# Copying the router's columns of the folded value weights with ScalarE instead of a second pair of DMAs, and the order of the SBUF tiles

## The reference

```python
nx = layer_norm(x) * gamma + beta
q, k, v = nx @ Wq, ctx @ Wk, ctx @ Wv
weights = softmax(q k^T * H**-0.5)                 # [b, t, 64]
evidence = weights @ v
combined = concat([nx, evidence, anchor], -1)      # 768 features
router_probs = softmax(combined @ router_W + router_b)
h = silu(combined @ e_w1[e] + e_b1[e])             # three experts, 512 each
routed = sum_e router_probs[e] * (h @ e_w2[e] + e_b2[e])
g = sigmoid(silu(combined @ gate_w1 + gate_b1) @ gate_w2 + gate_b2)
out = x + g * (routed @ out_w + out_b)
```

## Time and profile before

| | us |
|---|---|
| median of 3 runs | 432.08 (431.96 to 432.52) |
| the profiled execution's own time | 431.96 |
| its span, first to last instruction | 430.1 |

### The profile page before, as it was taken

One profiled execution on the slowest core, in us unless ns is written; L12 is line 12 of the kernel. 1 busy time (PEld: TensorE's weight loads), 2 busy tenths in 40 slices (PEclk: granted clock), 3 DMA queues, 4 the chain that ended last, 5 costly groups with the idle time before them and its releaser, 6 DMA issues.

```text
span 430.1 us, 5791 instructions
## 1 busy us (share of the span) xinstructions
PE 424.5 (99%) x1940; PEld 346.5 (81%) x1940; DVE 317.0 (74%) x591; ACT 245.0 (57%) x373; POOL 105.7 (25%) x95
## 2 busy tenths in 40 slices
PE   8999999999999999999999999999999999999995
PEld 7578888878888888887888888888888888888885
DVE  3778689899787767785677777785678757664366
ACT  3366855867555656464665657464565657455340
POOL 2300321142215032402125032402025022402440
PEclk9999999999999999999999999999999999999999
DMA  8989868027537334632633525622632525122302
GB/s 241 246 195 228 193 213 172 12 72 200 129 93 189 107 65 111 169 82 67 146 99 99 137 64 116 175 67 82 138 100 56 137 60 115 36 63 81 77 0 49
DMA packets 79586, 50.31 MB, mean 117 GB/s; under 512 B 58270, under 2 KB 68038, under 8 KB 79558
## 3 DMA queue, kind: packets, MB, share of 16 engines
q1 hardware_dynamic: 77552, 48.09, 45.4%
q0 software_dynamic: 800, 1.58, 1.4%
q10 hardware_dynamic: 1206, 0.29, 0.3%
HBM read 27.29 MB, written 7.93 MB: 82 GB/s over the span
## 4 chain that ended last, share of the span: by engine, by line
PE 97%; DVE 2%; issue 1%; ACT 0%; DVEq 0%
PE bank L624 40%; PE bank L871 34%; PE bank L856 12%; PE bank L644 2%; PE bank L741 2%; PE bank L669 1%; PE bank L711 1%; PE bank L648 1%; PE bank L697 1%; PE bank L755 1%; PE bank L777 0%; DVE work L1422 0%; PE bank L656 0%; DVE quad L1424 0%; PE bank L749 0%
## 5 line engine op out<-in xcount | busy, mean ns | idle before, releaser
L624 PE MATMUL bank<-nx,w1n 128*128 128x512 f32 x672 | 171.6, 391 | 0.0
L1087 ACT ACTIVATE hf<-bank,zb 128x512 f32<-128x512 f32 x112 | 77.3, 690 | 131.4 <-PE bank L856 129.2
L624 PEld LDWEIGHTS bank<-nx,w1n 128*128 128x128 f32 x672 | 125.8, 188 | 27.0 <-issue 0.5
L871 PE MATMUL bank<-h,w 128*128 128x512 f32 x552 | 140.3, 389 | 0.0
L871 PEld LDWEIGHTS bank<-h,w 128*128 128x128 f32 x552 | 103.6, 188 | 21.8
L1453 DVE TENSOR_TENSOR h<-hf,h 128x512 fp32r<-128x512 f32 x111 | 85.5, 774 | 45.4 <-ACT h L1091 43.4
L1091 ACT ACTIVATE h<-bank,zb 128x512 fp32r<-128x512 f32 x111 | 75.8, 682 | 0.0
L856 PE MATMUL bank<-wT,vw 128*128 128x512 f32 x224 | 69.7, 392 | 0.0
L856 PEld LDWEIGHTS bank<-wT,vw 128*128 128x128 f32 x224 | 41.9, 188 | 9.3 <-issue 0.5
L1490 POOL TENSOR_TENSOR xq<-xq,quad 128x512 f32<-128x512 f32 x14 | 19.6, 1421 | 106.5 <-DVE quad L1160 106.5
L1505 POOL TENSOR_TENSOR work<-work 128x512 f32<-128x512 f32 x14 | 18.9, 1350 | 70.6 <-DVE work L1370 59.1
(11 more groups left out here) (160 smaller groups left out, 452.6 us busy)
## 6 DMA issues: line engine op xcount, KB each, us to landing
vw<-vw_pair SPq DMA_DIRECT2D x48, 256.0 KB, 3.7
xn<-in_x_dram SPq DMA_DIRECT2D x8, 512.0 KB, 4.6
p_bc<-prob_dram SPq DMA_DIRECT2D x8, 512.0 KB, 5.1
xq<-in_x_dram SPq DMA_DIRECT2D x32, 128.0 KB, 2.5
out_dram<-xq SPq DMA_DIRECT2D x28, 128.0 KB, 2.8
stage<-in_L_xcond_e_w_dram SPq DMA_DIRECT2D x24, 128.0 KB, 4.3
xhat_dram<-xn SPq DMA_DIRECT2D x6, 512.0 KB, 2.8
quad<-xhat_dram SPq DMA_DIRECT2D x24, 128.0 KB, 2.5
```

Source lines behind the costliest of these rows:

```text
L624: mm = pe.matmul(dst, lhs(a), rhs(c), start=first and i == 0, stop=last and i == n - 1)
L871: mm = pe.matmul(bank[place][:, :], lhs, h_tile(s, a), start=c == 0 and i == 0, stop=c == COUNT[g] - 1 and i == 2)
L1087: act.activation(hf[:, s % 2, :], z, ACT.Silu, bias=zb[:, j, b:b + 1]).then_inc(s_h, 1)
```

## The change

Three things. First, `vw` gets the 4 router columns too, and the two DMAs of `load_vw` for g = 0 copy them along with the gate's 256 columns. The two DMAs that wrote `vr` go, with SP's wait for `s_lg`. Second, a new step `vr_copy(b)` on ScalarE waits for `s_dup[0]` and `s_lg` and copies the 8 values of each partition from `vw` to `vr`. It is put behind `w_hi(0)` ahead of the loop, and for the other batches into slot 12 of b = 0 (behind the slot's work, ahead of `w_hi`) and slot 10 of every later b (ahead of the slot's Silus; behind `w_hi` where that stands in the same slot). TensorE's `logits` waits for the copy, and its evidence matmuls read `vw` 4 columns further right. Third, nearly all SBUF tiles are named, and so placed, in another order.

```diff
@@ tiles
+        xn = sb("xn", [PART, NT, H])
         NJ = T // QROWS
-        w1n = sb("w1n", [PART, 2, KC, NCOL], F32R)
-        w2 = sb("w2", [PART, 2, E * EB, H], F32R)
-        gw2 = sb("gw2", [PART, 2, GB, H], F32R)
-        vw = sb("vw", [PART, 2, NCOL], F32R)
-        nx = sb("nx", [PART, 2, 2, KC, T], F32R)
-        h = sb("h", [PART, HRING, 2, T], F32R)
-        wT = sb("wT", [PART, 2, T], F32R)
...
+        w1n = sb("w1n", [PART, 2, KC, NCOL], F32R)
+        vw_pair = sb("vw_pair", [PART, 2, VCOL], F32R)
+        vw = sb("vw", [PART, 2, VCOL], F32R)
+        w2 = sb("w2", [PART, 2, E * EB, H], F32R)
+        gw2 = sb("gw2", [PART, 2, GB, H], F32R)
+        qkr = sb("qkr", [PART, 2, KC, B, SC], F32R)
+        h = sb("h", [PART, HRING, 2, T], F32R)
+        hf = sb("hf", [PART, 2, T])
+        nx = sb("nx", [PART, 2, 2, KC, T], F32R)
+        nxf = sb("nxf", [PART, KC, T])
+        soft = sb("soft", [NP, T])
+        wfull = sb("wfull", [NP, T])
+        vr = sb("vr", [PART, SC], F32R)
+        wT = sb("wT", [PART, 2, T], F32R)
@@ plans (only what is new in them)
-        FIRST_PLAN: 12: ["whi+"]
+        FIRST_PLAN: 12: ["vr+","whi+"]
-        SECOND_PLAN: 10: ["wlo"]
+        SECOND_PLAN: 10: ["vr", "wlo"]
-        THIRD_PLAN, EVEN_PLAN, ODD_PLAN: 10: ["whi"]
+        THIRD_PLAN, EVEN_PLAN, ODD_PLAN: 10: ["whi", "vr"]
+                    "vr": ((of,), {"act": ["vr_copy"]}, {}),
@@ load_vw, on SP
                 for half in range(2):
-                    sp.dma_start(vw[NP * half:NP * (half + 1), :, COLS[g]].bitcast(F32),
-                                 vw_pair[r:r + NP, :, RP + COLS[g].start:RP + COLS[g].stop].bitcast(F32))\
-                      .then_inc(s_dup[g], 16)
-                if g == 0:
-                    if b >= 1:
-                        sp.wait_ge(s_lg, b)
-                    for half in range(2):
-                        sp.dma_start(vr[NP * half:NP * (half + 1), NP:SC].rearrange("p (a c) -> p a c", a=2).bitcast(F32),
-                                     vw_pair[r:r + NP, :, 0:RP].bitcast(F32)).then_inc(s_vr, 16)
+                    sp.dma_start(vw[NP * half:NP * (half + 1), :, VCOLS[g]].bitcast(F32),
+                                 vw_pair[r:r + NP, :, VCOLS[g]].bitcast(F32)).then_inc(s_dup[g], 16)
@@ logits and first_layer_evidence, on TensorE
-                pe.wait_ge(s_vr, 32 * (b + 1))
+                pe.wait_ge(s_vr, b + 1)
-                    mm = pe.matmul(bank[ZB[s % 3]][:, :], vw[:, part, j * PART:(j + 1) * PART],
+                    mm = pe.matmul(bank[ZB[s % 3]][:, :], vw[:, part, RP + j * PART:RP + (j + 1) * PART],
@@ ScalarE
+            def vr_copy(b):
+
+                act.wait_ge(s_dup[0], 32 * (b + 1))
+                if b >= 1:
+                    act.wait_ge(s_lg, b)
+                act.copy(vr[:, NP:SC].rearrange("p (a c) -> p a c", a=2), vw[:, :, 0:RP]).then_inc(s_vr, 1)
@@ pair_hi, on ScalarE
-                    if g == 0:
-                        act.wait_ge(s_vr, 32 * 2 * pair)
@@ ahead of ScalarE's loop over the slots
             w_hi(0)
+            vr_copy(0)
             act.activation(silu_of_one[:, :], ones8[:, 0:1], ACT.Silu)
             pair_hi(0, 2)
```

More of the change, by code:

```diff
@@ L79, in sem @@
             return es.enter_context(nc.semaphore(name))
+        xn = sb("xn", [PART, NT, H])
         NJ = T // QROWS
[L83 to L94, removed]
-        w1n = sb("w1n", [PART, 2, KC, NCOL], F32R)
-        w2 = sb("w2", [PART, 2, E * EB, H], F32R)
-        gw2 = sb("gw2", [PART, 2, GB, H], F32R)
-        vw = sb("vw", [PART, 2, NCOL], F32R)
-        nx = sb("nx", [PART, 2, 2, KC, T], F32R)
-        h = sb("h", [PART, HRING, 2, T], F32R)
-        wT = sb("wT", [PART, 2, T], F32R)
-        hf = sb("hf", [PART, 2, T])
-        nxf = sb("nxf", [PART, KC, T])
-        xn = sb("xn", [PART, NT, H])
         xq = sb("xq", [PART, NJ, H // QUADS])
         quad = sb("quad", [PART, NJ, H // QUADS])
[L108 to L114, removed]
         xhat0 = quad[:, :, :].rearrange("p j c -> p (j c)").rearrange("p (t h) -> p t h", t=NT)
@@ L117, in build @@
         xq_blocks = xq[:, :, :].rearrange("p j (k a) -> p k j a", k=KC)
+        w1n = sb("w1n", [PART, 2, KC, NCOL], F32R)
+        VCOL = RP + NCOL
+        VCOLS = [slice(RP + c.start if g else 0, RP + c.stop) for g, c in enumerate(COLS)]
+        vw_pair = sb("vw_pair", [PART, 2, VCOL], F32R)
+        vw = sb("vw", [PART, 2, VCOL], F32R)
+        w2 = sb("w2", [PART, 2, E * EB, H], F32R)
+        gw2 = sb("gw2", [PART, 2, GB, H], F32R)
+        SC = NP + 2 * RP
+        qkr = sb("qkr", [PART, 2, KC, B, SC], F32R)
+        HRING = 3
+        h = sb("h", [PART, HRING, 2, T], F32R)
         warm = h[:, HRING - 1, LO, 0:2 * PART]
+        hf = sb("hf", [PART, 2, T])
+        nx = sb("nx", [PART, 2, 2, KC, T], F32R)
+        nxf = sb("nxf", [PART, KC, T])
         nxf_blocks = nxf[:, :, :].rearrange("p k (j b) -> p k j b", b=QROWS)
+        soft = sb("soft", [NP, T])
         soft_blocks = soft[:, :].rearrange("p (j a) -> p j a", a=QROWS)
         logit_blocks = soft_blocks[0:QROWS, :, :]
+        wfull = sb("wfull", [NP, T])
+        vr = sb("vr", [PART, SC], F32R)
+        wT = sb("wT", [PART, 2, T], F32R)
         b2o = sb("b2o", [PART, KC, E])
         gb2_half = sb("gb2_half", [PART, KC])
+        p_bc12 = sb("p_bc12", [PART, E - 1, T])
+        ident = sb("ident", [PART, PART])
+        ones8 = sb("ones8", [8, PART])
         silu_of_one = sb("silu_of_one", [8, 1])
+        NROWS = NB + 4 * KC + E * KC + B * KC
         rows = hf[0:NROWS, 0, 0:PART]
@@ L129, in build @@
         gw2_raw = hf[:, 1, :].rearrange("p (k n) -> p k n", k=GB)
+        cols = sb("cols", [PART, NROWS])
         C_B1, C_GAMMA, C_BETA = 0, NB, NB + KC
@@ L134, in build @@
         C_OUTB = C_GB2 + KC
+        zb = sb("zb", [PART, NB, B])
         wr = sb("wr", [PART, 3 * KC, RP])
@@ L141, in build @@
         mv = sb("mv", [PART, NT, 2])
+        ve = sb("ve", [PART, NT])
         rstd = sb("rstd", [PART, NT])
         minus_half = sb("minus_half", [PART, NT])
+        part_red = sb("part_red", [NP, 2, NJ])
         upper_red = sb("upper_red", [QROWS, 2, NJ])
+        whole_red = sb("whole_red", [NP, 2, NJ])
         red3 = sb("red3", [QROWS, 4, NJ])
@@ L264, in stage_of @@
             return u % STAGES, (s_stage[u % STAGES], 16 * transfers)
-        FIRST_PLAN = {0: ["b2o","ewT0"], 2: ["b2+","rm_+"], 3: ["owhi","fold0","owlo","shi2"], 4: ["px_","ewt1","ehi1","zb2+","slo2+","elo1+","pr_"], 6: ["ewt2","fold1","split3","ehi2","elo2+"], 7: ["xt","vwp3"], 8: ["fold2","nx","vsplit1"], 9: ["zb3+","sc+","vsplit3"], 10: ["vsplit2"], 11: ["ex+","wg"], 12: ["whi+"], 13: ["wlo+"]}
-        SECOND_PLAN = {0: ["lg_+"], 1: ["px_+"], 2: ["pr_", "vsplit0"], 3: ["vsplit4"], 4: ["nx"], 6: ["vwp0", "sc+"], 7: ["vwp1+"], 8: ["ex", "wg"], 9: ["vwp2+"], 10: ["wlo"], 11: ["whi", "vwp3"], 12: ["lg+"], 13: ["pr"]}
-        THIRD_PLAN = {0: ["px_"], 2: ["nx"], 5: ["sc"], 7: ["wg"], 8: ["ex"], 9: ["wlo"], 10: ["whi"], 11: ["lg"],
+        FIRST_PLAN = {0: ["b2o","ewT0"], 2: ["b2+","rm_+"], 3: ["owhi","fold0","owlo","shi2"], 4: ["px_","ewt1","ehi1","zb2+","slo2+","elo1+","pr_"], 6: ["ewt2","fold1","split3","ehi2","elo2+"], 7: ["xt","vwp3"], 8: ["fold2","nx","vsplit1"], 9: ["zb3+","sc+","vsplit3"], 10: ["vsplit2"], 11: ["ex+","wg"], 12: ["vr+","whi+"], 13: ["wlo+"]}
+        SECOND_PLAN = {0: ["lg_+"], 1: ["px_+"], 2: ["pr_", "vsplit0"], 3: ["vsplit4"], 4: ["nx"], 6: ["vwp0", "sc+"], 7: ["vwp1+"], 8: ["ex", "wg"], 9: ["vwp2+"], 10: ["vr", "wlo"], 11: ["whi", "vwp3"], 12: ["lg+"], 13: ["pr"]}
+        THIRD_PLAN = {0: ["px_"], 2: ["nx"], 5: ["sc"], 7: ["wg"], 8: ["ex"], 9: ["wlo"], 10: ["whi", "vr"], 11: ["lg"],
                       12: ["pr"], 13: ["px"]}
-        EVEN_PLAN = {2: ["nx"], 5: ["sc"], 7: ["wg"], 8: ["ex"], 9: ["wlo"], 10: ["whi"], 11: ["lg"], 12: ["pr"],
+        EVEN_PLAN = {2: ["nx"], 5: ["sc"], 7: ["wg"], 8: ["ex"], 9: ["wlo"], 10: ["whi", "vr"], 11: ["lg"], 12: ["pr"],
                      13: ["px"]}
         ODD_PLAN = {2: ["nx"], 3: ["vwp0"], 4: ["vwp1+"], 5: ["sc"], 7: ["vwp2", "wg"], 8: ["ex"], 9: ["wlo"],
-                    10: ["whi"], 11: ["lg", "vwp3"], 12: ["pr"], 13: ["px"]}
+                    10: ["whi", "vr"], 11: ["lg", "vwp3"], 12: ["pr"], 13: ["px"]}
         PLANS = (FIRST_PLAN, SECOND_PLAN, THIRD_PLAN)
@@ L1029, in v_hi @@
                 act.copy(w1v_hi[n], w1v[:, :, VCOLS[n]]).then_inc(s_vhi, 1)
-            steps = {"v_hi": v_hi, "nx_hi": nx_hi, "exp": exp, "w_hi": w_hi, "exp_router": exp_router,
+            steps = {"v_hi": v_hi, "nx_hi": nx_hi, "exp": exp, "w_hi": w_hi, "vr_copy": vr_copy, "exp_router": exp_router,
                      "pair_hi": pair_hi, "fold_hi": fold_hi, "ew_hi": ew_hi, "out_hi": out_hi, "gate_tanh": gate_tanh, "gate_factor": gate_factor,
```

## The result

The changed kernel takes 435.85 us (median of 4, 435.70 to 436.06) where the kernel before takes 432.02 us in the same job. The ratio is 1.0087, with a 95% interval from 1.0069 to 1.0104: 3.8 us slower. It lies outside the predicted range, on the side to which I gave 12%.

What follows compares the result with a forecast made beforehand. TensorE's dense matmul stream was taken as the bound, busy 424.5 of 430.1 us. 431.96 + 0 + 0 + 0 = 431.96 us; with the median before 0.12 above it, the forecast was 432.1, range 431.0 to 433.4.

Steps and rivals of the forecast that it cites:

- the side to which I gave 12%: Whole kernel: measurably slower, by a late ScalarE or by tile placement, 12%; no measurable change had 80%, faster 8%.
- the DMAs that go: SP: 16 DMAs into `vr` vanish, 9.7 us of SP in all, but TensorE never waits for them: 0 us.
- the copy that comes: ScalarE: 8 copies of about 0.20 us fit into idle time; 0 us, 1.6 us if every copy were exposed.
- Rival 1: ScalarE, slot 12 of batch 0 and its like: wait or copy exceeds 0.6 us of room, TensorE waits; 433.7 us, 5%.
- first-in-first-out rule: ScalarE's queue is strictly in order, so a late `vw` would stop the Silus feeding TensorE; here it costs nothing.
- The new order of tiles: All TensorE matmuls: new address distances between operands were taken to leave 226.7 ns a matmul unchanged, 0 us.
- The wider `vw`: Evidence matmuls: rows 16 bytes longer, weights begin 16 bytes further on, count and width stay; no cost, 0 us.
- rival 2: TensorE: operands at new offsets lengthen matmuls; 433.2 us on the evidence matmuls alone, 439.8 on all; 7%.
- upper end (+7.7 us): All 1544 slot matmuls taking 5.0 ns more through placement: +7.7 us.
- 231.7 ns lasts into tiles that are well placed: Chain: 6 pair-product matmuls and the 6 that follow took 231.7 ns each; taken as evidence against placement.

Runs made afterwards that it cites:

- g2: The change with the old tile order and 64 columns ahead in `vw`, so main operands stand at multiples of 256 bytes: 432.01 against 432.22 us before, 0.9997.
- h5: The kernel before with the pair product's operands, `w1v_lo` included, put at multiples of 256 bytes (except group 0): 431.38 against 432.39 us, 0.9980.
- e1: The kernel before with the changed kernel's tile order only, no copy, the DMAs into `vr` kept: +5.2 us, ratio 1.0117.
- e3: The kernel before with 64 unused bytes ahead of all tiles: +0.7 us, ratio 1.0022, slot 3183.3 ns against 3183.2.
- g3: The kernel before with 32 unused bytes ahead of all tiles: +0.3 us, ratio 1.0019, slot 3183.5 ns against 3183.2.
- f and h runs: Kernel before, `nx` alone 32, 64, 128, 256 bytes later: +5.9, +6.0, +4.2, -0.5 us; `nx`, `h`, `wT` 64, 128, 192 later: +2.6, +8.6, +9.9 us.
- g1: The kernel before with `w1n` and `nx` both 64 bytes further on, other operands at multiples of 256 bytes: +4.0 us, ratio 1.0089.
- g4: The kernel before with the pair product's operands, all but `w1v_lo`, put at multiples of 256 bytes: 431.54 against 432.22 us, 0.9973.

## Why the prediction was wrong

**Right:** the DMAs that go (0 us) and the copy that comes (0 us; 0.198 us each against 0.20 taken; no wait on a DMA; TensorE's waits as before). `g2` shows both together at 0.9997. Rival 1, a ScalarE that is late, didn't happen: 0.41 us of the 0.49 of idle time at slot 12 were still left. For the first-in-first-out rule that I cited from the Trainium skill ("TensorE: Matmul & The Clock Gate") the case shows no cost.

**Wrong:** the step "The new order of tiles", taken as 0, and with it "The wider `vw`", also taken as 0. They are worth 3.9 us, and rival 2 came true. The mechanism was named and its upper end (+7.7 us) worked out from a row, but I left it out of the range. Three arguments led there, and each fails in a way that can be learnt from. The first rests on one row; the chain of the kernel before has this one too:

```profile
153.36 0.92 PE bank L644 x4
```

- "`qkr`'s distance is no multiple of 512, and its matmuls take 227.5 ns". That is one batch of eight, the last. A block of `qkr` is 288 bytes, so its distance from `nx` is 32 bytes times the batch's number, modulo 256: 224 bytes in that row. The same trace has longer ones. The row above is batch 3 (96 bytes), and the starts of its six matmuls give 228 229 234 227 228 229 ns. In batch 5 (160 bytes) they give 229 232 227 226 229 231, and the next four 235 229 232 231, with nothing longer ahead. Batches 2 and 7 (64 and 224 bytes) show nothing, 226 or 227 ns each. I took one row as a witness for all, and the trace in hand spoke against it.
- "231.7 ns lasts into tiles that are well placed, so it isn't placement". It is: a disturbance goes on for some four matmuls behind its cause, and `h5` removed it by placing the operands of the pair product. In the kernel before they stood, modulo 256, at 160 (`vT_hi`), 128 (`vT_lo`, `stage_hi`) and 112 or 128 (`w1v_lo`), and those of the slots at 0.
- "`w1v_lo` is off by 16 bytes and the starts are 0.23 us apart". The row rounds to 0.01 us, and 0.2267 and 0.2317 both print as 0.23; the effect is 2 to 3% of a matmul. Nor was the `stage_hi` beside it well placed: it stood 32 bytes off its weights, `vT_hi`. Sums over twelve, or starts to the nanosecond, were needed.

The two-port rule that I cited against collisions (the Trainium skill, "TensorE: Matmul & The Clock Gate", "Step-by-step: what each phase is for": loading the next weights takes no bandwidth from the running matmul) is no ground for taking placement as free: with all moving operands of a slot 64, 128 and 192 bytes off, a matmul takes 2.2, 6.4 and 6.7 ns more. Of the 11 ns by which 226.7 exceeds the 215.7 that the same page of the Trainium skill states ("Wait — 56ns, not 53.3ns?") no placement tried gave any back.

**Shown:** the loss is placement (`e1`, `g2`); a common shift costs nothing (`e3`, `g3`), a distance of 32, 64, 128 or 192 bytes between weights and moving operand does, one of 256 doesn't (f and h runs); neighbours take part (`g1`, and the matmul ahead of the pair product). **Only argued:** that the load of the next weights and the running matmul's reads get into each other's way inside the chip. **Open:** the price of a distance, above all why 64 bytes cost less when all moving operands are off than when `nx` alone is, and 128 bytes more; why a `logits` matmul whose operands stand right is followed by longer ones; and how the 3.9 us of the changed kernel follow from its distances.

## What to carry to other kernels

In a kernel bound by a dense stream of fp32r matmuls as here, the places of the SBUF tiles are part of the tuning: keep stationary and moving operands, those of neighbouring matmuls too, a multiple of 256 bytes apart (64 bytes for all alike still cost 0.6%), and treat any added column, pad or new order as a change to every matmul. Test such an edit by itself before reading the rest of a diff. And when nothing waits but the bound engine is busy longer, compare the starts of its instructions, position by position.

## What the runs showed of the hardware

- fp32r matmuls of 512 columns with 128-column weights, back to back with the clock at 2.4 GHz (granted clock 0.999), start every 226.6 ns (median slot / 14) when weights and moving operands are a multiple of 256 bytes apart, and every 228.9, 233.0 and 233.4 ns when all moving operands are 64, 128 and 192 bytes off. Moving everything by 32 or 64 bytes changes nothing.
- The next matmul's weights count too: the well-placed matmul ahead of a pair product took 237 ns with that product's operands at 160 and 128 modulo 256 and 227 ns with them at 0 (`g4`).
- One misplaced kind of matmul can lengthen the next ones: with `wT` alone 32 bytes off, the intervals were 236, 230, 230, 233, 231, then 226 to 227 ns. In `g4` a single matmul took 233 ns and the next 227.
- A ScalarE copy of 128 x 8 values in fp32r takes 0.192 to 0.218 us.
